# Value product of an attention kernel: two fp16 halves in three products, in place of one fp32 product

## What is computed

```python
qh, kh, vh = split_heads(layernorm(x) @ Wq), split_heads(ctx @ Wk), split_heads(ctx @ Wv)
dots = einsum('bhid,bhjd->bhij', qh, kh) * SCALE        # masked, causal
attn = softmax(dots)
out = einsum('bhij,bhjd->bhid', attn, vh)
x = x + tanh(g_xattn) * (out @ Wo + bo)
x = x + tanh(g_ffn) * ffn(layernorm(x))                 # quantised feed-forward, untouched by the change
```

## Time and profile before

| | |
|---|---|
| runs | 1625.19, 1627.03, 1629.18 us; median 1627.03 us |
| profiled execution, its own time | 1626.47 us |
| its span | 1624.6 us |
| PE, DVE, ACT, POOL busy, share of the span | 94%, 85%, 77%, 64% |
| attention stage | first 1050 us; PE busy 788 of 800 us between 100 and 900 us |

### The profile page before, as it was taken

How to read it: one execution, slowest core, us unless ns; L and a number is a source line. 1 busy time by engine, 2 the same in 40 slices (tenths; PEclk the granted TensorE clock), 3 DMA queues, 4 the chain that set the end, 5 groups by cost and what they waited for, 6 DMA issues and landing times. The chain is left out here.

```text
span 1624.6 us, 38058 instructions
## 1 busy us (share of the span) xinstructions
PE 1530.6 (94%) x12556; PEld 1251.8 (77%) x12556; DVE 1385.1 (85%) x2247; ACT 1253.4 (77%) x3222; POOL 1033.8 (64%) x1004
## 2 busy tenths in 40 slices
PE   7899999999999999999999999789989997995998
PEld 5787887877877878878778788677767776775887
DVE  7888888888888888888888889878887998998996
ACT  5887887888778778878887787566758998885674
POOL 3988988888888889888888888600006664740000
PEclk9999999999999999999999999999998999997999
DMA  6554445444444544454444445369957884755664
GB/s 195 118 127 103 105 106 122 104 92 115 106 105 103 126 102 105 107 121 104 92 115 106 105 103 98 86 205 344 321 215 262 282 287 153 276 227 187 218 214 145
DMA packets 347365, 252.23 MB, mean 155 GB/s; under 512 B 287792, under 2 KB 317616, under 8 KB 344368
## 3 DMA queue, kind: packets, MB, share of 16 engines
q1 hardware_dynamic: 347312, 251.58, 55.1%
HBM read 105.25 MB, written 76.02 MB: 112 GB/s over the span
## 5 line engine op out<-in xcount | busy, mean ns | idle before, releaser
L496 ACT ACTIVATE prob<-masked,neg_max 128x128 f32<-128x128 f32 x1024 | 397.6, 391 | 35.1 <-DVE neg_max L662 31.6
L431 POOL TENSOR_TENSOR prob_parts<-prob,prob_parts 128x512 f16<-128x512 f32 x254 | 310.3, 1241 | 2.7 <-ACT prob_parts L504 1.6
L426 POOL TENSOR_TENSOR prob<-prob,scaled 128x512 f32<-128x512 f32 x256 | 271.6, 1061 | 20.1
L660 DVE TENSOR_TENSOR masked<-score,mask_add 128x512 f32<-128x512 f32 x256 | 174.6, 682 | 74.0 <-PE score L963 67.9
L504 ACT ACTIVATE prob_parts<-prob 128x512 f16<-128x512 f32 x254 | 159.0, 627 | 75.6 <-POOL prob L426 71.7
L496 ACT ACTIVATION_READ_ACCUMULATOR prob<-masked,neg_max 128x1 f32 x1024 | 193.3, 189 | 0.0
L662 DVE TENSOR_REDUCE neg_max<-masked 128x4 f32<-128x512 f32 x256 | 175.6, 686 | 8.8
L438 POOL TENSOR_TENSOR probT<-turn 128x512 f32<-128x512 f16 x125 | 173.2, 1386 | 0.0
L1723 POOL TENSOR_SCALAR xThi<-n_x 128x1024 fp32r<-128x1024 int16 x15 | 43.8, 2919 | 202.9 <-DMA n_x<-n_x_d 166.8
L976 PE MATMUL y<-wo_hi,o_hi 128*128 128x256 f32 x508 | 148.3, 292 | 15.9 <-DVE o_lo L667 15.2
L424 POOL TENSOR_TENSOR scaled<-rsums,pscale 128x4 f32<-128x4 f32 x256 | 66.4, 259 | 124.0 <-DVE rsums L654 123.9
(11 more groups left out here) (249 smaller groups left out, 4485.5 us busy)
## 6 DMA issues: line engine op xcount, KB each, us to landing
gate<-gate_d SPq DMA_DIRECT2D x30, 768.0 KB, 4.3
n_x<-n_x_d SPq DMA_DIRECT2D x25, 512.0 KB, 4.9
gate_d<-stage SPq DMA_DIRECT2D x8, 1536.0 KB, 5.5
n_u_d<-w_raw SPq DMA_DIRECT2D x16, 768.0 KB, 4.1
stage<-n_u_d SPq DMA_DIRECT2D x16, 768.0 KB, 6.0
gate_d<-gate SPq DMA_DIRECT2D x7, 1536.0 KB, 5.5
x_in<-in_x SPq DMA_DIRECT2D x16, 512.0 KB, 3.9
ctx_in<-in_ctx_columns SPq DMA_DIRECT2D x16, 512.0 KB, 4.8
```

Of the source, the lines that this page charges most:

```text
L426: gp.tensor_tensor(prob[:, h], prob[:, h], scaled[:, h, :].rearrange("p (b o) -> p b o", o=1).broadcast_to([P, NB, P]), ALU.mult).then_inc ...
L431: gp.tensor_tensor(prob_parts[:, h, 1], prob[:, h].rearrange("p b k -> p (b k)"), prob_parts[:, h, 0], ALU.subtract).then_inc(prob_low, 1)
L496: nc.scalar.activation(prob[:, h, b, :], masked[:, h, b, :], ACT.Exp, bias=neg_max[:, h, b:b + 1], accum_out=psums[:, h, b:b + 1]).then_in ...
L660: nc.vector.tensor_tensor(masked[:, h], score[h][:], mask_add[:], ALU.add).then_inc(masked_done, 1)
```

## The change

The summing of the turned halves goes (`join_prob`, `join_second`, `probT`). PE takes the halves out of `turn` as fp16, and the values as two fp16 halves in `v16`: high x high, high x low, low x high, 24 one-pass products for each unit where there were eight fp32 ones. So that fp16 holds the values, each group gets a scale: `ctx_top` takes the row maxima of the context, `value_bound` multiplies them on PE with the row maxima of Wv (an upper bound for every value), `value_scale` makes the factor and its inverse, `output_unit` puts the factor into the scalar that `residual` multiplies with.

A value now takes two instructions in each of the steps 0 to 6: ACT scales and rounds to the high half, then DVE subtracts it from the scaled value (a `scalar_tensor_tensor`), and DVE's end frees the bank. `turn_prob` waits for the product that last read the slot, where it waited for the sum.

```diff
-        v_sb = sb("v_sb", [P, NB, INNER])
+        v16 = sb("v16", [P, NB, 2, 2, VH], F16)
...
-                wait(sp, probT_copied[h], u - 1)
+                wait(sp, pv_done, u - 1)
                 sp.dma_start_transpose(out=turn[:, u % 2, h], in_=prob_parts[:, h].rearrange("p e n -> p (e n)")).then_inc(prob_turned[h][u % 2], 16)
...
-            def join_second(u, slot, times):
...
-                if old:
-                    join_second(u - 3, (c + 1) % 2, NC // 2 * g + (c - 1) // 2)
...
-                if new and c > 2:
+                if new:
                     for i, n in jobs_of(c, "v"):
                         b, before = nth(g, i)
+                        if n == 0:
+                            act.wait_ge(v_scaled, 4 * g + 3)
                         act.wait_ge(projected[b], before + 1)
-                        nc.scalar.activation(v_sb[:, n % NB, VH:2 * VH], proj[b][:], ACT.Copy).then_inc(copied[b], 1)
+                        nc.scalar.activation(v16[:, n % NB, n // NB, 0], proj[b][:], ACT.Copy, scale=v_mul[:, 0:1]).then_inc(v_high, 1)
...
             def values(g, c):
                 for i, n in jobs_of(c, "v"):
                     b, before = nth(g, i)
-                    dve.wait_ge(projected[b], before + 1)
-                    nc.vector.tensor_copy(v_sb[:, n % NB, 0:VH], proj[b][:]).then_inc(copied[b], 1)
+                    dve.wait_ge(v_high, NC * g + n + 1)
+                    nc.vector.scalar_tensor_tensor(v16[:, n % NB, n // NB, 1], proj[b][:], v_mul[:, 0:1], v16[:, n % NB, n // NB, 0],
+                                                   ALU.mult, ALU.subtract).then_inc(copied[b], 1)
+
+            def ctx_top(g):
+
+                dve.wait_ge(ctx_loaded, 16 * (g + 1))
+                nc.vector.tensor_reduce(c_top[:], ctx_in[:], X, ALU.max, apply_absolute_value=True).then_inc(v_scaled, 1)
+
+            def value_scale(g):
+
+                dve.wait_ge(v_bound, g + 1)
+                nc.vector.tensor_scalar(v_unit[:], trans[:, 0, 0:1], 1.0 / VMAX, VTINY, ALU.mult, ALU.max).then_inc(v_scaled, 1)
+                dve.wait_ge(v_scaled, 4 * g + 2)
+                nc.vector.reciprocal(v_mul[:], v_unit[:]).then_inc(v_scaled, 1)
+                dve.wait_ge(v_scaled, 4 * g + 3)
+
+            def output_unit(g):
+
+                if isinstance(g, int) and g == 0:
+                    dve.wait_ge(bo_ready, 2)
+                nc.vector.tensor_tensor(y_unit[:], tg_small[:], v_unit[:], ALU.mult).then_inc(v_scaled, 1)
+                dve.wait_ge(v_scaled, 4 * g + 4)
...
                     attended_low(u - 4)
-                if old:
-                    join_prob(u - 3, 0, (c + 1) % 2, NC // 2 * g + (c - 1) // 2)
...
+                if c == 4:
+                    output_unit(g)
+                if c == 6 and more:
+                    ctx_top(g + 1)
...
+                if isinstance(g, int) and u == 0:
+                    value_scale(0)
                 if soft:
                     reciprocals(u - 1, 1)
-                if c < 3:
-                    values(g, c)
+                values(g, c)
+                if nxt:
+                    value_scale(g + 1)
                 if c == 4 and after_first:
                     second_moments(g - 1)
...
             w_low_part(2)
+            dve.wait_ge(w_loaded[5], 16)
+            nc.vector.tensor_reduce(w_top[:], w_stage(2), X, ALU.max, apply_absolute_value=True)
+            ctx_top(0)
             w_low_part(3)
...
-                        last = nc.tensor.matmul(pv[h * HD:(h + 1) * HD, b, :], v_sb[:, b, c * P + h * HD:c * P + (h + 1) * HD],
-                                                probT[:, h, b, :], start=True, stop=True)
+                    for n, (m, t) in enumerate(((0, 0), (0, 1), (1, 0))):
+                        for h in range(2):
+                            at = c % NB * P + h * HD
+                            last = nc.tensor.matmul(pv[h * HD:(h + 1) * HD, b, :], v16[:, b, c // NB, m, at:at + HD],
+                                                    turn[:, slot, h, t * NB + b, :], start=(n == 0), stop=(n == 2))
                 last.then_inc(pv_done, 1)
+
+            def value_bound(g):
+
+                pe.wait_ge(v_scaled, 4 * g + 1)
+                for k in range(KC):
+                    last = nc.tensor.matmul(trans[:, 0, 0:1], c_top[:, k:k + 1].broadcast_to([P, P]), w_top[:, k:k + 1],
+                                            start=(k == 0), stop=(k == KC - 1))
+                last.then_inc(v_bound, 1)
...
+                if first:
+                    value_bound(0)
                 if nxt:
                     transpose_in(g, *ts[0])
...
                 if nxt:
                     transpose_in(g, *ts[1])
+                    value_bound(g + 1)
```

More of the change, by code:

```diff
@@ L41 @@
 PSCALE = 32768.0
+VMAX = 60000.0
+VTINY = 1e-30
 def split(hi, lo):
@@ L130, in attention @@
         kT = sb("kT", [P, T])
-        v_sb = sb("v_sb", [P, NB, INNER])
+        v16 = sb("v16", [P, NB, 2, 2, VH], F16)
+        v_stage = v16[:].rearrange("p b h n i -> p (b h n i)").bitcast(F32).rearrange("p (b i) -> p b i", b=NB)
+        w_top, c_top = sb("w_top", [P, KC]), sb("c_top", [P, KC])
+        v_unit, v_mul, y_unit = (sb(n, [P, 1]) for n in ("v_unit", "v_mul", "y_unit"))
         masked = sb("masked", [P, 2, NB, P])
@@ L202, in attention @@
         xres_loaded = sem("xres_loaded")
-        probT_copied = [sem(f"probT_copied{h}") for h in range(2)]
+        v_high = sem("v_high")
+        v_scaled = sem("v_scaled")
+        v_bound = sem("v_bound")
+        last_turned = sem("last_turned")
         pv_done = sem("pv_done")
@@ L573, in _ @@
             attended(U - 2)
-            act.wait_ge(last_step, 1)
             act.wait_ge(pv_done, U - 1)
-            nc.scalar.activation(probT[:, 0], trans[:], ACT.Copy).then_inc(probT_copied[0], 1)
-            for n in range(4):
+            for h in range(2):
+                act.wait_ge(last_step, h + 1)
+                nc.scalar.activation(turn[:, 1, h, 0:NB], trans[:], ACT.Copy).then_inc(v_high, 1)
+                if h == 0:
+                    ffn_high_part(0)
+            for n in range(1, 4):
                 ffn_high_part(n)
@@ L642, in w_low_half @@
                     last.then_inc(w_ready, 1)
[L644 to L649, removed]
             def reciprocals(u, h):
@@ L821, in _ @@
             for h in range(2):
-                nc.vector.memset(score[h][:], 0.0).then_inc(score_zero, 1)
+                nc.vector.memset(score[h][:], 0.0)
             w_low_part(0)
@@ L840, in _ @@
             attended_low(U - 4)
-            for h in range(2):
-                join_prob(U - 3, h, 1, U // 2 - 1)
             maxima(U - 1, 1)
@@ L847, in _ @@
             attended_low(U - 3)
-            for h in range(2):
-                join_prob(U - 2, h, 0, U // 2)
             attended_low(U - 2)
             weight_values(2, 1)
-            ffn_low_part(0)
-            dve.wait_ge(last_step, 2)
-            dve.wait_ge(pv_done, U - 1)
-            nc.vector.tensor_copy(probT[:, 1], trans[:]).then_inc(probT_copied[1], 1)
+            for h in range(2):
+                dve.wait_ge(v_high, NC * G + h + 1)
+                nc.vector.tensor_tensor(turn[:, 1, h, NB:2 * NB], trans[:], turn[:, 1, h, 0:NB], ALU.subtract).then_inc(last_turned, 1)
+                if h == 0:
+                    ffn_low_part(0)
             for n in range(1, 4):
@@ L864, in _ @@
                 dve.wait_ge(last_step, n + 3)
-                nc.vector.scalar_tensor_tensor(x1[:, rows], y[:, rows], tg_small[:, 0:1],
+                nc.vector.scalar_tensor_tensor(x1[:, rows], y[:, rows], y_unit[:, 0:1],
                                                xres[:, rows], ALU.mult, ALU.add).then_inc(x1_ready, 1)
@@ L937, in scores_free, with times_v @@
                     wait(pe, masked_done, 2 * (u - 1) + h + 1)
-            def times_v(u, c, then=None):
+            def times_v(u, c, slot, times, then=None):
                 for h in range(2):
-                    pe.wait_ge(probT_copied[h], u + 1)
+                    if times is None:
+                        pe.wait_ge(last_turned, 2)
+                    else:
+                        pe.wait_ge(prob_turned[h][slot], 16 * times)
                 wait(pe, out_split, u)
@@ L1012, in step @@
                 if old:
-                    times_v(u - 3, co, (g, c, u) if new else None)
+                    times_v(u - 3, co, (c + 1) % 2, NC // 2 * g + (c - 1) // 2, (g, c, u) if new else None)
                 if new:
```

25 lines of the change are left out of this document (10 added, 15 removed).

## The result

The changed kernel takes 1695.15 us (median of four runs, 1691.12 to 1695.93) where the kernel before, beside it, took 1626.13: a ratio of 1.042, 95% interval 1.039 to 1.044. The prediction was 1655.0 us with a range of 1600 to 1684: the sign held, the size did not. The profiled execution took 1695.32 us, its span is 1693.5 us, 68.9 more than before.

The account below looks back on a forecast made before the run. PE at 2.4 GHz was taken to set the pace in the attention stage, o_lo its one late input. Terms -23 + 7 + 27 + 6 + 15 - 6 + 3 = +29 us on 1626.5 gave 1655 us, range 1600 to 1684.

Parts of the forecast that it names:

- Product, -23: pv on PE: 24 one-pass fp16 products take 0.84 us for 1.02, 0.18 us less in each of 128 steps, -23 us.
- Step 4 to 5, +1.8 a group: Moments behind DVE's subtraction are held by POOL, o_lo late, y waits 2.0 us for 0.2; 15 groups, +27 us.
- Steps 5 to 6 and 6 to 7, +0.4 and +1.0: second_norm and normalise behind DVE's added work meet POOL; y waits 0.4 and 1.2 us for o_lo; +6 and +15 us.
- Step 7 to 0, -0.4: PE arrives later, so step 0's wait for o_lo shrinks, value_scale taking part back: -0.4 us a group, -6 us.
- The bound, +0.44 a group: value_bound's two fp32 products on PE in step 7 take 0.44 us, 15 groups, +7 us.
- Start and tail, +3: Two DVE reduces ahead of wq_lo, first value product held, a subtraction in the tail: +3 us (0 to +5).
- the first (the port doesn't bind): Rival: DVE's short instructions slip in between POOL's, waits of steps 5, 6 and 7 vanish: 1602 us, chance 0.27.

Follow-up runs that it names:

- two_products: ctx_early without the third product (low half of values by high half of probabilities), 16 products a unit for 24: 1576.72 us.
- moments_ahead: The changed kernel with second_moments of step 4 put ahead of the second reciprocal, where POOL is idle: 1648.97 us, 1.0125 of the kernel before.
- low_short: The changed kernel in its own order, POOL's low half of the probabilities cut from 512 columns to 32: 1607.01 us, 0.987 of the kernel before.
- all_ahead: The changed kernel with moments, second_norm's second half and normalise ahead of the second reciprocal, context's reduce split over steps 5 and 6: 1609.08 us, 0.988 of the kernel before.
- scale_step0: all_ahead with value_scale moved from the end of step 7 into step 0, ahead of the second reciprocal: 1605.58 us, 0.987 of the kernel before.
- no_bound: all_ahead with a constant scale, without maxima, bound products, value_scale and per-group output scalar: 1594.96 us, 0.982 of the kernel before.
- ctx_early: scale_step0 with the start rearranged and the context's reduce halves in steps 1 and 5, none in step 6: 1589.96 us, 0.977 of the kernel before.
- clock_filler: The changed kernel with 14 identity transposes on PE ahead of y in step 5 and 10 in step 7: 1675.17 us, 1.028 of the kernel before.

## Why the prediction was right and wrong

By its steps, against the 68.9 us between the two spans:

- *Product, -23.* Right in kind, too small: steps without a wait are 0.26 us shorter, 128 of them 33 us. A pair costs 0.055 us for the 0.058 taken, and pv to score is 0.79 us for 0.84. By the rule of the Trainium skill (TensorE: Matmul & The Clock Gate, section Part 3: Packing small matmuls) that a load overlaps a running matmul only in other row groups (it names a background weight buffer as another way), a pair would be 0.113 us by the prediction's estimate; two_products, with both heads on all 128 rows in the two column halves, disagrees. Of the rows that the prediction set against that rule, those of pv bear on it; those of the scores don't, as a head takes only 64 rows there (64*64).
- *Step 4 to 5, +1.8 a group.* Right, with its mechanism: v_sum and mean were held to the ends of POOL's two low halves, vare ended 534.78, y waited 1.88 us where I took 2.0; moments_ahead and low_short remove it from either side.
- *Steps 5 to 6 and 6 to 7, +0.4 and +1.0.* The waits for o_lo came out as taken, 0.41 and 1.19 us, but the second by luck: 1.2 was set between 2.1 us (DVE and POOL alternate) and 0.4 (they don't), and they did alternate: x_in was held by each low half in turn (1.25 us twice). PE also waited some 0.4 us for x_in ahead of that. By the ledger, less the product's 0.26 and the bound's 0.44, the steps cost 0.6 and 1.4 us, so these two terms were 9 us too small in 15 groups.
- *Step 7 to 0, -0.4.* Wrong: I let PE's lateness use up the wait of step 0. Late steps don't shorten it: it is 9.96 us in all_ahead too, where steps 5 and 6 have no wait. value_scale came on top (0.44 us by scale_step0). Step 0 is 9.96 us where the forecast's terms make 9.32, 15 by 0.64: 10 us.
- *The bound, +0.44 a group.* The products are as forecast, 0.44 us to pv in a step 7 at full clock (0.78 in the group shown above, where the clock had fallen):

```profile
490.49 0.50 PE L982 MATMUL trans<-w_top,c_top 128*128 128x1 f32 x4
490.93 0.86 PE L974 MATMUL pv<-turn,v 128*64 128x128 f16 x24
```

  The reduce and the bound together cost 1.06 us a group in no_bound, in part through the late reciprocal in step 6 (ctx_early, which takes the reduce out of step 6, gets 0.55 of it back), a path that I did not follow.
- *Start and tail, +3.* Mis-sized: the first score of group 1 comes 8.9 us later (95.4 for 86.5), the stretch from group 15's first score to the end is 3.2 us longer. The start is known only to some 5 us: moments_ahead and clock_filler, which are the same up to there, reach group 1 at 100.4 and 99.9 us. PE waits for the context's maxima, and its bound stands ahead of the first value product:

```profile
18.67 0.60 PE L982 MATMUL trans<-w_top,c_top 128*128 128x1 f32 x4 [4.07 <-DVE c_top L685]
```

  The first value product starts 1.9 us late (19.14 for 17.24); the rest of the 3.5 us by which the first scores are late comes at the 1.2 GHz level (19.8 to 23.2 us). The clock fell twice more in group 0, where it did not fall in the kernel before.

- *The missing term.* The step that failed most is the one that is not in the sum: I priced every wait at its own length on PE at the 2.4 GHz level. The earlier trace rows shows the clock at 1.00, and the attention stage of the kernel before gave no reason for another price: PE's longer waits outside the loop, up to 2.7 us, were followed by no fall, these two among them (the falls of that trace come from 1063 us on, with waits of 2.8 us and more):

```profile
34.18 0.90 PE L963 MATMUL score<-kT,qT 64*64 64x128 f32 x32 [1.81 <-ACT kT L511]
...
1037.74 0.39 PE L976 MATMUL y<-wo_hi,o_hi 128*128 128x256 f32 x1 [2.70 <-DVE o_lo L667]
```

  In the changed kernel the clock fell to the 1.2 GHz level in 13 steps of groups 1 to 14: in nine behind the 1.88 us of step 5, in four behind the waits of step 7 (0.4 us for x_in, then 1.19 for o_lo). clock_filler puts that at 20 us, and its 1675 us lie inside the predicted range: it is the falls that took the time out of it.

Together: groups 1 to 14 at the forecast's 1.8 us make 25 us; measured are 35.1 without the falls, 21.7 for the falls, and 12.1 for start and tail (their own falls included), which is the 68.9. Of the rivals, the first (the port doesn't bind) is refuted by v_sum and mean; its time, 1602, is nonetheless near what low_short and all_ahead reach, which take POOL out of the way.

## What to carry to other kernels

Where one engine's small instructions stand ahead of the result that the pacing engine waits for, their place in the order relative to the other engine's long ones can be worth more than the edit itself: seven tiny instructions moved to where POOL stands idle were 46 us here, clock falls included. A change that frees an engine often needs its order made anew before the gain shows: the same three moves lost time in the kernel before and won it here. And where a change puts waits of 1 to 2 us on PE, count beside the wait a chance that the clock falls behind it.

## What was not expected of the hardware

- Two waits of the same length, 1.88 us ahead of 536.89 and 1.89 us ahead of 401.50, ended differently: the first left the clock at 1.00, the second brought 0.53 from 402 to 404 us. What decides it is not shown here, and the length of the wait alone does not: 1.19 us (with 0.4 just ahead) was followed by a fall in four steps, 2.70 us in the kernel before by none. 14 transposes of the identity in the wait (1.69 us of work, then 0.34 us idle) kept it at 1.00 in every group.
- A fall in step 7 costs little: that group took 66.5 us for 66.3, since step 0 behind it shrank from 9.96 to 8.75, where its wait for o_lo was absorbed. A fall in step 5 costs 2.0 to 2.4 us (68.3 to 68.7 us for the group), with step 6 lengthened too.
- Some DVE instructions that meet POOL are held to the end of POOL's instruction, one POOL instruction for each: v_sum to the first low half, mean to the second, x_in likewise; m_sq and v_eps, started as POOL was stopping, took 0.15 us. Others are not held: masked took 0.68 us beside a low half (542.83), the context's reduce 1.19 us beside prob (546.15).
